# Another order for the front, the first step and the read-out of a four-part layer, and thirteen filling products in three waits

## What is computed

```python
# 1. memory MLP (two layers, 64 -> 128 -> 64) trained by gradient over the T = 16 rows, then read with q
q = l2norm(xn @ Wq)                                  # xn = layer norm of x
def step((params, mom), x_t):                        # per batch item, 64 wide, 16 tokens a step
    k, v = l2norm(x_t @ Wk), x_t @ Wv
    lr, forget, eta = means of sigmoids of x_t @ w_*
    g = grad(mean((mlp(params, k) - v) ** 2))
    mom = eta * mom - lr * g
    params = params * (1 - forget) + mom
x = x + mlp(mean over batch of params_T, q)
# 2. mixture of 8 experts, top 2, each gelu(xe @ W1 + b1) @ W2 + b2 with its own layer norm scale and shift
# 3. three convolution scans (1x1, 3x3, 1x1) over 64 channels
# 4. a gated recurrence of 64 units over 256 steps, batch 4
```

## Time and profile before

| | us |
|---|---|
| median of three runs | 595.57 |
| lowest, highest | 589.94, 596.36 |
| profiled execution | 592.88 |
| its span, first to last instruction | 591.1 |
| PE busy in the span | 537.3 (91%) |
| DVE, ACT, POOL busy | 285.9, 217.6, 104.3 |
| mean granted clock of PE | 0.963 |

### The profile page before, as it was taken

How to read it: one execution, slowest core, us unless ns; L and a number is a source line. 1 busy time by engine, 2 the same in 40 slices (tenths; PEclk the granted TensorE clock), 3 DMA queues, 4 the chain that set the end, 5 groups by cost and what they waited for, 6 DMA issues and landing times.

```text
span 591.1 us, 10757 instructions
## 1 busy us (share of the span) xinstructions
PE 537.3 (91%) x3798; PEld 310.1 (52%) x3798; DVE 285.9 (48%) x1320; ACT 217.6 (37%) x1084; POOL 104.3 (18%) x103
## 2 busy tenths in 40 slices
PE   6799999999987999898799999999999999999996
PEld 4598888888744433377354444444444444444443
DVE  2636666666644744701734444444444444444443
ACT  1425555555423634010133333333333333333332
POOL 3227777777810000000000000000000000000000
PEclk9759999999988999999889999999999999999998
DMA  7400000000000000000000000000000000000000
GB/s 216 202 2 0 2 2 1 2 2 1 2 0 1 0 1 2 0 1 0 1 2 1 1 2 1 2 1 2 2 1 2 1 2 1 1 2 0 2 2 19
DMA packets 2871, 7.12 MB, mean 12 GB/s; under 512 B 1404, under 2 KB 1985, under 8 KB 2625
## 3 DMA queue, kind: packets, MB, share of 16 engines
q1 hardware_dynamic: 2818, 6.44, 3.1%
HBM read 6.18 MB, written 0.26 MB: 11 GB/s over the span
## 4 chain that ended last, share of the span: by engine, by line
PE 52%; DVE 24%; ACT 16%; issue 7%; POOL 1%; DVEq 0%; POOLq 0%
PE bk L652 14%; DVE bk L1143 8%; ACT gi L813 8%; DVE mem L1146 7%; ACT bk L817 6%; PE bk L538 4%; PE bk L609 4%; PE bk L556 2%; PE bk L463 2%; PE bk L422 2%; PE bk L444 2%; PE bk L432 2%; PE bk L362 1%; PE bk L355 1%; PE bk L394 1%
## 5 line engine op out<-in xcount | busy, mean ns | idle before, releaser
L668 PE MATMUL bk<-idle 128*64 128x512 bf16 x720 | 201.1, 385 | 0.0
L652 PEld LDWEIGHTS bk<-mem,lvh 65*64 65x64 f32 x1536 | 81.0, 138 | 145.4 <-DVE mem L1146 144.1
L652 PE MATMUL bk<-mem,lvh 65*64 65x4 f32 x1536 | 103.8, 207 | 23.4 <-DVE mem L1146 4.3
L813 ACT ACTIVATE gi<-bk 128x4 f32<-128x4 f32 x256 | 45.0, 176 | 151.6 <-PE bk L652 151.6
L1143 DVE TENSOR_TENSOR_SCAN bk<-gi 64x12 f32<-64x12 f32 x256 | 47.6, 186 | 107.0 <-ACT gi L813 107.0
L668 PEld LDWEIGHTS bk<-idle 128*64 128x64 bf16 x720 | 61.3, 112 | 22.9 <-issue 1.2
L1146 DVE SCALAR_TENSOR_TENSOR mem<-og,bk 64x4 f32<-64x4 f32 x256 | 38.4, 150 | 53.7 <-ACT bk L817 53.7
L817 ACT ACTIVATE bk<-bk 64x4 f32<-64x4 f32 x256 | 36.6, 143 | 40.8 <-DVE bk L1143 40.3
L1150 DVE SCALAR_TENSOR_TENSOR gi<-mem,bk 64x4 f32<-64x4 f32 x255 | 39.1, 153 | 8.8
L815 ACT ACTIVATE og<-bk 64x4 f32<-64x4 f32 x256 | 42.8, 167 | 0.1
L919 DVE TENSOR_TENSOR mem<-mem,bk 128x256 f32<-128x256 f32 x64 | 26.8, 421 | 18.1 <-PE bk L355 12.0
(11 more groups left out here) (266 smaller groups left out, 727.0 us busy)
## 6 DMA issues: line engine op xcount, KB each, us to landing
cw<-in_cw SPq DMA_DIRECT2D x1, 3456.0 KB, 11.2
w<-in_w SPq DMA_DIRECT2D x1, 520.0 KB
mem<-in_memw SPq DMA_DIRECT2D x1, 512.0 KB, 3.2
w<-in_w SPq DMA_DIRECT2D x1, 512.0 KB
xm<-in_xm SPq DMA_DIRECT2D x1, 256.0 KB, 2.6
xs<-in_x SPq DMA_DIRECT2D x1, 256.0 KB, 3.6
out<-xs SPq DMA_DIRECT2D x1, 256.0 KB, 2.0
consts<-in_consts SPq DMA_DIRECT2D x1, 134.0 KB, 2.5
```

The source lines that it names most:

```text
L652: return nc.tensor.matmul(bk[row:row + D, 2 * (s // CH % 2) + k, c:c + B], lvh[:, g, :], hist[:, s, :], start=False, stop=True, skip_group ...
L668: nc.tensor.matmul(bk[0:D, 5, 0:FILL_N], idle[:, 0:D], idle[:, 128:128 + FILL_N], start=True, stop=True)
L813: nc.scalar.activation(gi[:, 2:2 + 3 * B:3], bk[:, bank, cols], ACT.Tanh).then_inc(sem("in_gate"), 1)
```

## The change

- **Fillers**: three products of 512 columns between the first transposes and the wait for xnT, five between the first and second c1 product, five ahead of step 0.
- **Front**: POOL clears `warm` first; ACT waits for that alone ahead of its first table. POOL clears w1g and x2A and scales w1 (L294 before) ahead of the loop. K is squared, summed and rooted ahead of q, in two halves. The c1 products and their copies move from behind the read-out to here, and the K transposes wait for the copy of c1b (their banks are the same). SP loads c1p and c1last earlier.
- **First step**: gate products, DVE's gate chain, the q transposes and the qq copies move into step 0. The gram products become eight, seven of 128 columns and one of 64.
- **Read-out and behind**: the sum over the batch is split by weight, with a signal for each. The experts' bias is made by sixteen products of one column each into b1p, which the gelu adds; w1row and its copy go. DVE and ACT share the copies to t1T and x2A, and two experts' gelus come ahead of the router's tanh on ACT.

```diff
+                                (c1p[:, :, :], "c1p", "ld_c1"), (c1last[:, :], "c1last", "ld_c1"),
...
-            nc.gpsimd.memset(idle[:, :], 0.0)
-            nc.gpsimd.memset(xnT[:, :], 0.0).then_inc(sem("idle"), 1)
+            nc.gpsimd.memset(warm[:, :], 0.0).then_inc(sem("warm"), 1)
+            nc.gpsimd.memset(idle[:, :], 0.0).then_inc(sem("idle"), 1)
+            nc.gpsimd.memset(xnT[:, :], 0.0).then_inc(sem("xnT_zero"), 1)
             nc.gpsimd.memset(pads[:, :, :], 0.0)
             nc.gpsimd.memset(sc0[:, :, :], 0.0)
             for t in (*img, *zim):
                 nc.gpsimd.memset(t[:, :, :], 0.0)
-            nc.gpsimd.memset(warm[:, :], 0.0).then_inc(sem("cleared"), 1)
+            nc.gpsimd.memset(x2A[:, :], 0.0)
+            nc.gpsimd.memset(w1g[:, :, :], 0.0).then_inc(sem("cleared"), 1)
+            pool.wait_ge(sem("cleared"), 1)
+            pool.wait_ge(sem("ld_w1"), 48)
+            nc.gpsimd.tensor_tensor(w1g[0:D, :, :], w1[0:D, :, :], wide(lng[:, :], H), ALU.mult).then_inc(sem("w1g"), 1)
...
             pe.wait_ge(sem("ld_a"), 48)
+            busy(3, 7)
             pe.wait_ge(sem("xnT"), 2)
...
+            pe.wait_ge(sem("ld_c1"), 32)
+            nc.tensor.matmul(bk[0:D + 1, 0, 0:D + 1], c1p[:, 2, :], c1last[:, :], start=True, stop=True).then_inc(sem("c1_ps"), 1)
+            busy(5, 1)
+            pe.wait_ge(sem("c1"), 1)
+            nc.tensor.matmul(bk[0:D + 1, 1, 0:D + 1], c1p[:, 1, :], c1a[:, :], start=True, stop=True).then_inc(sem("c1_ps"), 1)
             pe.wait_ge(sem("KK"), 1)
+            pe.wait_ge(sem("c1"), 2)
             for n in range(NT):
                 ins = nc.tensor.transpose(bk[:, n // 4, (n % 4) * 128:(n % 4 + 1) * 128], KK[:, n, :], ident)
                 if n % 4 == 3:
                     ins.then_inc(sem("kkT_ps"), 1)
-            pe.wait_ge(sem("ld_g"), 32)
-            pe.wait_ge(sem("glin"), 1)
-            for g in range(3):
-                ins = nc.tensor.matmul(bk[:, 2, g * B * T:(g + 1) * B * T], gsel[:, g, :], glin[:, :], start=True, stop=True)
-            ins.then_inc(sem("gate_ps"), 1)
-            pe.wait_ge(sem("QV"), 1)
-            for n in range(NT):
-                ins = nc.tensor.transpose(bk[:, 4 + n // 4, (n % 4) * 128:(n % 4 + 1) * 128], QV[:, n, :], ident)
-                if n % 4 == 3:
-                    ins.then_inc(sem("qqT_ps"), 1)
+            pe.wait_ge(sem("gS"), 2)
+            nc.tensor.matmul(bk[0:D + 1, 2, 0:D + 1], c1p[:, 0, :], c1b[:, :], start=True, stop=True).then_inc(sem("c1_ps"), 1)
+            busy(5, 3)
...
-                    for k in range(1, T):
-                        n = (k - 1) // 2
-                        ins = nc.tensor.matmul(bk[:, 6 - k // 8, (k % 8) * TB:(k % 8 + 1) * TB], kblk[:, n * 128:(n + 1) * 128],
-                                               kblk[:, k * TB:(k + 1) * TB], start=True, stop=True)
-                        if k % 8 == 7:
+                    pe.wait_ge(sem("ld_g"), 32)
+                    pe.wait_ge(sem("glin"), 1)
+                    pe.wait_ge(sem("vneg"), 2)
+                    for g in range(3):
+                        ins = nc.tensor.matmul(bk[:, 7, 256 + g * B * T:256 + (g + 1) * B * T], gsel[:, g, :], glin[:, :],
+                                               start=True, stop=True)
+                    ins.then_inc(sem("gate_ps"), 1)
+                    for n in range(NT):
+                        w = min(128, (T - 1 - 2 * n) * TB)
+                        ins = nc.tensor.matmul(bk[:, 6 - n // 4, n % 4 * 128:n % 4 * 128 + w], kblk[:, n * 128:(n + 1) * 128],
+                                               kblk[:, (2 * n + 1) * TB:(2 * n + 1) * TB + w], start=True, stop=True)
+                        if n % 4 == 3:
                             ins.then_inc(sem("gram_ps"), 1)
+                    pe.wait_ge(sem("QV"), 1)
+                    pe.wait_ge(sem("gS"), 2)
+                    for n in range(NT):
+                        ins = nc.tensor.transpose(bk[:, 3 + n // 4, (n % 4) * 128:(n % 4 + 1) * 128], QV[:, n, :], ident)
+                        if n % 4 == 3:
+                            ins.then_inc(sem("qqT_ps"), 1)
...
+                    pe.wait_ge(sem("qq"), 2)
...
             pe.wait_ge(sem("FW"), 1)
...
+            pe.wait_ge(sem("FW"), 2)
...
+            pe.wait_ge(sem("FW"), 3)
...
+            pe.wait_ge(sem("FW"), 4)
...
-            pe.wait_ge(sem("ld_c1"), 32)
-            nc.tensor.matmul(bk[0:D + 1, 2, 0:D + 1], c1p[:, 2, :], c1last[:, :], start=True, stop=True).then_inc(sem("c1_ps"), 1)
             pe.wait_ge(sem("ld_w1"), 48)
-            for e in range(E):
-                ins = nc.tensor.matmul(bk[64:65, 4 + e // 2, (e % 2) * H:(e % 2 + 1) * H], lnb[:, e:e + 1], w1[:, e, :],
+            for k in range(E * HC):
+                ins = nc.tensor.matmul(bk[:, 4, k:k + 1], w1[:, k // HC, k % HC * 128:(k % HC + 1) * 128], lnb[:, k // HC:k // HC + 1],
                                        start=True, stop=True)
-            ins.then_inc(sem("w1row_ps"), 1)
-            pe.wait_ge(sem("c1"), 1)
-            nc.tensor.matmul(bk[0:D + 1, 3, 0:D + 1], c1p[:, 1, :], c1a[:, :], start=True, stop=True).then_inc(sem("c1_ps"), 1)
-            pe.wait_ge(sem("c1"), 2)
-            nc.tensor.matmul(bk[0:D + 1, 2, 0:D + 1], c1p[:, 0, :], c1b[:, :], start=True, stop=True).then_inc(sem("c1_ps"), 1)
-            pe.wait_ge(sem("c1"), 3)
+            ins.then_inc(sem("b1_ps"), 1)
             busy(AFTER[1], 7)
...
-            act.wait_ge(sem("cleared"), 1)
+            act.wait_ge(sem("warm"), 1)
             table(ACT.Sqrt)
             root(1)
+            act.wait_ge(sem("xnT_zero"), 1)
             for n in range(2):
                 act.wait_ge(sem("xnT_ps"), n + 1)
                 nc.scalar.copy(xnT[0:D, n * 512:(n + 1) * 512], bk[0:D, n, :]).then_inc(sem("xnT"), 1)
             act.wait_ge(sem("qk_ps"), 1)
             qk = bk[:, 4:6, :].rearrange("p k (n c) -> p k n c", n=4)
-            nc.scalar.activation(qksq[:, :, :].rearrange("p (k n) c -> p k n c", n=4), qk, ACT.Square).then_inc(sem("qksq"), 1)
+            for a in (1, 0):
+                nc.scalar.activation(qksq[:, :, a * D:(a + 1) * D].rearrange("p (k n) c -> p k n c", n=4), qk[:, :, :, a * D:(a + 1) * D],
+                                     ACT.Square).then_inc(sem("qksq"), 1)
             act.wait_ge(sem("qk_sq"), 1)
-            nc.scalar.activation(qkr[:, :, :], qkv2[:, :, :], ACT.Sqrt).then_inc(sem("qk_n"), 1)
+            nc.scalar.activation(qkr[:, 1, :], qkv2[:, 1, :], ACT.Sqrt).then_inc(sem("qk_n"), 1)
+            act.wait_ge(sem("c1_ps"), 1)
+            nc.scalar.copy(c1a[:, :], bk[0:D + 1, 0, 0:D + 1]).then_inc(sem("c1"), 1)
+            act.wait_ge(sem("qk_sq"), 2)
+            nc.scalar.activation(qkr[:, 0, :], qkv2[:, 0, :], ACT.Sqrt).then_inc(sem("qk_n"), 1)
+            act.wait_ge(sem("c1_ps"), 2)
+            nc.scalar.copy(c1b[:, :], bk[0:D + 1, 1, 0:D + 1]).then_inc(sem("c1"), 1)
             table(ACT.Gelu_apprx_tanh)
...
+            act.wait_ge(sem("c1_ps"), 3)
+            nc.scalar.copy(c1a[:, :], bk[0:D + 1, 2, 0:D + 1]).then_inc(sem("c1"), 1)
+            act.wait_ge(sem("cleared"), 1)
...
-            for k, dst in enumerate((c1a, c1b, c1a)):
-                act.wait_ge(sem("c1_ps"), k + 1)
-                nc.scalar.copy(dst[:, :], bk[0:D + 1, 2 + k % 2, 0:D + 1]).then_inc(sem("c1"), 1)
-                if k == 0:
-                    act.wait_ge(sem("w1row_ps"), 1)
-                    act.wait_ge(sem("w1g"), 1)
-                    nc.scalar.copy(w1g[D:D + 1, :, :].rearrange("p (k n) h -> p k (n h)", k=4), bk[64:65, 4:8, :]).then_inc(sem("w1row"), 1)
             root(2)
+            act.wait_ge(sem("b1_ps"), 1)
+            nc.scalar.copy(b1p[:, :], bk[:, 4, 0:E * HC]).then_inc(sem("b1p"), 1)
             root(3)
...
+            act.wait_ge(sem("XT_ps"), 2)
+            nc.scalar.copy(t1T[64:128, 512:1024], bk[64:128, 3, :]).then_inc(sem("t1T"), 1)
+            nc.scalar.copy(x2A[0:D, 512:1024], bk[0:D, 3, :]).then_inc(sem("x2A"), 1)
...
+            for k, a in enumerate((1, 0)):
+                dve.wait_ge(sem("qksq"), k + 1)
+                link(nc.vector.tensor_reduce(qkr[:, a, :], qksq[:, :, a * D:(a + 1) * D], AX, ALU.add))
+                nc.vector.tensor_scalar(qkv2[:, a, :], qkr[:, a, :], 1e-24, None, ALU.max).then_inc(sem("qk_sq"), 1)
...
+            for k, (a, dst) in enumerate(((1, KK), (0, QV))):
+                dve.wait_ge(sem("qk_n"), k + 1)
+                link(nc.vector.reciprocal(qkr[:, a, :], qkr[:, a, :]))
+                newton(qkr[:, a, :], qkv2[:, a, :], nt[:, a * NT:(a + 1) * NT])
+                unit(dst[:, :, 0:D], a)
+                unit(dst[:, :, D:2 * D], a).then_inc(sem("KK" if a else "QV"), 1)
...
+                    dve.wait_ge(sem("gate_ps"), 1)
+                    link(nc.vector.tensor_copy(gat[:, :, :], bk[:, 7, 256:256 + 3 * B * T].rearrange("p (g s) -> p g s", g=3)))
...
```

(16 more changed lines are left out.)

93 lines of the change are left out of this document (38 added, 55 removed).

## The result

The changed kernel took 576.99 us (median of four executions, 573.73 to 579.59), the kernel before 595.97 on the same chip (four executions, 589.94 to 597.24). The ratio is 0.970, with a 95% interval of 0.961 to 0.978. The profiled execution is the fastest of the four, 573.73 with a span of 571.9.

The account below looks back on a forecast made before the run. PE, busy nearly everywhere, was taken as held back by half clock through step one and by waits in front and read-out. Terms 1.5 + 3.2 + 5.8 + 4.3 + 0.8 = 15.6 off 592.88 gave 577.3; forecast 578, range 572 to 587.

Parts of the forecast that it names:

- Front up to the K transposes: Kernel start to K transposes: earlier first transposes and faster q/k products gain 1.5 us, bounds 0 and 2.6.
- K transposes to step one: From K transposes to step one's first product: ACT's gate chain, then PE's fillers end last; 3.2 us gained, bounds 2.2 and 4.4.
- Step one: First step of the memory loop: 11.9 us in place of 17.7, so 5.8 gained, bounds 4.5 and 6.4.
- Read-out: Read-out: L481 waits only for PE's fillers, and the clock doesn't fall; 4.3 us gained, bounds 2.3 and 4.4.
- Norm behind it: Norm behind the read-out: DVE's 3.41 idle goes, but PE's fillers take most; 0.8 us more, bounds -2.1 and 3.7.
- The fillers are late next: Ahead of the XT transposes: PE's 14 fillers end last, and most of the 3.4 us is lost to them.
- POOL's scaling of w1 in front: Front: small DVE steps of the K norm could stand behind POOL's scaling, up to 0.8 us worse; left out of sum.
- Rival 1: Around the K transposes: the clock falls all the same, costing 4.5 us, so 582.5; chance 0.20.
- Rival 2: Ahead of XT: the fillers aren't late because the clock holds; 3.1 us better, 575; chance 0.10.
- rival 3: Front: the fillers don't raise the clock at all, second step at 48.1, time 592; chance 0.05.
- Rival 4: Recurrence: lower clock lasts longer, so slower; some 36 more half-clock steps eat the gain, 60 give 606; chance 0.03.
- The prediction's own sign of being wrong: Step one: the clock's record showing 0.50 there was named as a sign that the prediction is wrong.

Follow-up runs that it names:

- changed_again: The changed kernel, unaltered, run again on a second chip: 576.48 us against 590.25 for the kernel before, ratio 0.976.
- the run with both edits: Changed kernel with the five fillers ahead of the wait for ACT's gate values and POOL's w1 scaling right behind the memory loop: 579.67 us.
- the run with ten fillers: Changed kernel with 10 in place of 14 filling products ahead of the XT transposes: 576.16 us against the changed kernel's 576.48.

## Why the prediction was right, and which terms were not

The sum said 577.3 and 578 was forecast; 576.99 was measured. Term by term against the two profiled executions (591.1 - 571.9 = 19.2 in the spans; the sum had 15.6):

- *Front up to the K transposes*: 1.5 forecast, 19.82 - 18.26 = 1.56 measured, by luck. The q/k products start 1.53 earlier where 0.6 was taken, since the first transposes came 0.69 earlier and took 1.03 in place of 1.89. They took 1.63 less (2.05 for 3.68, 0.13 a row) where 0.9 was taken; the rise of the clock came, but at 5.78, ahead of them and not inside. From their end to the K transposes it then was 18.26 - 11.59 = 6.67 in place of 5.07, where "0 gained" was taken. The path over the copy of c1b came out as forecast (done at 16.88, 5.29 behind the products), but DVE's chain ended last, 2.24 of it through L891. These errors cancel.
- *K transposes to step one*: 3.2 forecast, 7.13 - 3.54 = 3.59 measured, within its bounds. The step named the wrong last one. "They hide behind the fillers by a little" is wrong in this execution: the K blocks end last, 0.99 behind the fillers. In changed_again, where the q/k products came later (10.38) and L891 stood for only 0.96, the K blocks are ready at 21.58, the fillers end at 22.09, and it is right; so it is with w1 behind the loop.
- *Step one*: 5.8 forecast, measured (44.66 - 26.95) - (33.00 - 21.80) = 17.71 - 11.20 = 6.5, 0.1 past the upper bound. By the starts of the products, the first ones took 1.56 (1.7 forecast), gate and gram products 2.65 (2.6), q's transposes 0.88 (1.09), and from L423 to the second step it was 33.00 - 26.89 = 6.11 (6.5). The granted clock in this execution was at 1.00 throughout.
- *The memory loop's other 15 steps*: nothing forecast, 115.72 - 115.15 = 0.6.
- *Read-out*: 4.3 forecast, 2.47 at the fillers and 1.51 behind them measured, 3.98. Both parts of the argument are confirmed by runs: with POOL out of the way the undivided addition takes 0.69, and with the pause gone the clock doesn't fall.
- *Norm behind it*: **the step that failed in size**, 0.8 forecast, 14.85 - 11.84 = 3.01 measured. "The fillers are late next" is right, and DVE's 3.41 are gone; the mis-sized term is the 16 one-column products. 5.4 was taken between 3.8 and 7.0; their 32 rows took 3.68, 0.115 a row, so the lower end held, with the clock at 1.00. In changed_again the clock fell at 161.69, inside them, and they took 4.64: then the forecast's value is nearer; in the run with both edits it fell at 159.54, soon behind their start, and they took 5.92.
- *POOL's scaling of w1 in front*: left out of the sum, with an estimate of up to 0.8. L891 took 2.41 beside it and 0.17 without it, and freeing it moved step one's first product from 21.80 to 19.63, in the run where the fillers didn't stand behind. So the estimate, which named no row, was too small by a factor of nearly three: one short instruction stood for the whole rest of POOL's 3.60. The Trainium skill (SBUF — State Buffer, Who interferes with whom) counts tensor_scalar too among the VectorE instructions that can take both ports, where its operands allow it, and says that the later of two then blocks fully; L891's 2.41 beside POOL and 0.17 without agree, though no row shows in which mode it ran. The prediction had looked only at instructions with two SBUF inputs.

The sum of 15.6 fell 3.6 short of the profiled pair. That 578 was so near is luck in part: on the first chip the gain in the medians was 19.0, but the kernel before stood there at 595.97, 2.3 above the 593.7 that the forecast started from. On the second chip the gain was 13.8, and by the means of the table it is 14.9, so the pair flatters the change: after's profiled execution was the fastest of its four, 3.3 below their median, with 13.7 us at 1.2 GHz. Rival 1 isn't a rival but a share of the executions: with the same front, two of four profiles show 0.50 in step one, and the second step there is 3.4 to 3.6 later (4.5 was priced up to the same place). The prediction's own sign of being wrong, 0.50 in step one, is met in those two. It should have stood in the forecast as a part of each median, not as a case with 0.20. Rival 2 (fillers not late) is out by the 1.09 above, and the run with ten fillers got 0.86 of it; rival 3 is out, since 157 us ran at 2.4 GHz. Rival 4 showed only in small: the recurrence's first stretch at the lower clock was 6.83 to 13.65 long in these profiles, not the 36 further steps that it needed.

What stays open: what decides in which of the equal executions the clock falls near 20, 23 or 160 us. No run varied that by itself, but the records show what goes with it, the moment of the first rise. In the nine profiles of the changed kernel and its variants with the thirteen fillers the ten fillers at the start begin at 1.45 each time, yet the first rise lies anywhere from 4.66 to 6.54. Where it lies at 4.66 to 5.05 (four profiles), the clock falls once more between 8.07 and 8.47, ahead of the q/k products; where it lies at 5.78 to 6.54 (five), it holds through them. Step one stayed at 2.4 GHz for the rises at 4.66, 4.68, 5.05 and 5.78, not for those at 5.01, 5.94, 6.01, 6.18 and 6.54. And the two profiles whose first rises are nearest, 4.66 with the scaling of w1 in the read-out and 4.68 in changed_again, have all their later falls within 0.03 of each other (161.67 and 161.69, 270.90 and 270.92), though that scaling stands at different places in them.

Open as well is why the clears in front, 3.65 us in the trace, leave the median of the kernel before where it was. By the means of the table, 1.1 of it is there once the clock is taken out; this is not shown in a second profile. And no run takes back the moved c1 chain, the moved gate products or the new bias alone: what these are worth is read from the two traces.

## What to carry to other kernels

Price a moved POOL operation at its whole length against each short DVE instruction of a kind that was seen to wait for it, not at some tenths: here a tensor_scalar and a tensor_tensor with two inputs in SBUF waited, a tensor_reduce did not. Where the operation lands is set by the load it waits for, so look for that row first. Where a clock falls in some executions and not in others, forecast the share of executions and read every edit twice: in the trace for the order of work, and over many executions for the time at the lower clock, since an edit of 2 to 3 us can vanish in the second. And price small PE products once for each clock from rows, and say where the clock is expected to change: the same 32 rows took 3.68, 4.64 and 5.92 us in three profiles.
